# Linear attention differences as products in PSUM, activation tables asked for early, and attention scores in 32-row quarters of the array

## The reference, cut to what matters

```python
def wkv_scan(w, k, v):              # over the tokens of an image, per channel
    def step(carry, kv):
        a, b, m = carry
        mm = maximum(m + w, kt)
        e1 = exp(m + w - mm)
        e2 = exp(kt - mm)
        return (e1 * a + e2 * vt, e1 * b + e2, mm), (a, b, m)
...
M  = maximum(maximum(mf, mb), kt + u)
y  = (exp(mf-M)*af + exp(mb-M)*ab + exp(kk-M)*vt) / (exp(mf-M)*bf + exp(mb-M)*bb + exp(kk-M))
x  = x + sigmoid(h @ Wr_a.T) * y @ Wo_a.T
kf = square(relu(ln(x) @ Wk_f.T))
x  = x + sigmoid(ln(x) @ Wr_f.T) * (kf @ Wv_f.T)
...
attn = softmax(einsum('bhqd,bhkd->bhqk', q, k) * 16**-0.5)
o = einsum('bhqk,bhkd->bqhd', attn, v)
x = x + (o @ proj_w.T + proj_b)
moe = sum over the two best experts e of gate_e * (gelu(ln(x) @ W1[e] + b1[e]) @ W2[e] + b2[e])
```

## Time and profile before

| | us |
|---|---|
| median of 3 runs | 376.76 |
| lowest, highest | 376.1, 378.78 |
| the profiled execution, its own time | 375.74 |
| its span from first to last instruction | 373.9 |
| PE busy | 317.3 (85%) |
| DVE busy | 217.0 (58%) |
| ACT busy | 196.9 (53%) |
| mean granted clock of PE | 0.926 of full |

### The profile page before, as it was taken

How to read it: one execution, slowest core, us unless ns; L and a number is a source line. 1 busy time by engine, 2 the same in 40 slices (tenths; PEclk the granted TensorE clock), 3 DMA queues, 4 the chain that set the end, 5 groups by cost and what they waited for, 6 DMA issues and landing times.

```text
span 373.9 us, 6947 instructions
## 1 busy us (share of the span) xinstructions
PE 317.3 (85%) x2285; PEld 271.7 (73%) x2285; DVE 217.0 (58%) x577; ACT 196.9 (53%) x507; POOL 85.7 (23%) x84
## 2 busy tenths in 40 slices
PE   8959960982199899999999989888899999999990
PEld 5947840672169688797798667778799978889890
DVE  1726998679997684605535467888333434333342
ACT  0053541932847547788966798414365434455550
POOL 9310002002000110100101000011425545546632
PEclk9988995697579999999999999999599999999997
DMA  8960000000000097175731224113213223323332
GB/s 270 356 190 3 0 0 0 3 0 0 0 0 2 1 296 237 38 206 151 227 100 28 75 61 154 39 32 100 69 12 57 45 43 52 53 50 53 53 36 25
DMA packets 23695, 29.13 MB, mean 78 GB/s; under 512 B 6010, under 2 KB 18762, under 8 KB 23658
## 3 DMA queue, kind: packets, MB, share of 16 engines
q1 hardware_dynamic: 19770, 23.85, 21.2%
q0 software_dynamic: 3888, 4.81, 8.1%
HBM read 23.54 MB, written 5.11 MB: 77 GB/s over the span
## 4 chain that ended last, share of the span: by engine, by line
PE 40%; DVE 23%; DMA 12%; issue 11%; ACT 8%; POOL 2%; DVEq 1%; POOLq 1%; SPq 0%; ACTq 0%
DMA out<-s,ffn 10%; PE banks L1284 8%; PE banks L1285 7%; PE banks L1515 4%; PE banks L1366 4%; PE banks L1314 3%; ACT patch L814 3%; PE banks L1498 2%; PE banks L1422 2%; PE banks L1393 2%; PE banks L1410 2%; DVE st L941 2%; PE banks L1329 2%; PE banks L1503 1%; POOL rs L618 1%
## 5 line engine op out<-in xcount | busy, mean ns | idle before, releaser
L618 POOL TENSOR_TENSOR rs<-va,consts 96x6 f32<-96x6 f32 (+1 forms) x16 | 19.1, 1193 | 213.4 <-DVEq L953 109.2
L1515 PE MATMUL banks<-arena,ffn 128*128 x240 | 42.8, 328 | 0.0
L650 POOL DMA_INDIRECT out<-s,ffn x20 | 31.8, 1589 | 45.4 <-DVE s L1241 39.2
L1515 PEld LDWEIGHTS banks<-arena,ffn 128*128 128x128 f32 x240 | 38.5, 190 | 0.5 <-issue 0.2
L874 ACT ACTIVATE ffn<-banks,chans 128x128 f32<-128x128 f32 x21 | 9.6, 458 | 53.6 <-PE banks L1488 50.9
L1329 PE MATMUL banks<-consts,xh 96*128 96x96 f32 (+1 forms) x96 | 12.6, 275 | 22.9 <-ACT xh L700 19.4
L1329 PEld LDWEIGHTS banks<-consts,xh 96*128 96x128 f32 (+1 forms) x96 | 10.0, 142 | 26.1 <-issue 24.7
L640 POOL DMA_INDIRECT vs<-xh_scratch,ffn x21 | 22.3, 1062 | 16.8 <-DVE ffn L1208 8.5
L1366 PE MATMUL banks<-rvw,ffn 128*96 128x192 f32 x144 | 25.4, 327 | 0.5 <-ACT ffn L786 0.5
L1314 PE MATMUL banks<-arena,patch 128*96 128x192 f32 x144 | 25.0, 327 | 0.3 <-DMA patch<-in_xp 0.3
L1314 PEld LDWEIGHTS banks<-arena,patch 128*96 128x96 f32 x144 | 23.0, 162 | 2.3 <-issue 1.9
(11 more groups left out here) (224 smaller groups left out, 771.4 us busy)
## 6 DMA issues: line engine op xcount, KB each, us to landing
arena<-in_w SPq DMA_DIRECT2D x8, 576.0 KB, 7.1
patch<-in_xp SPq DMA_DIRECT2D x12, 288.0 KB, 6.1
arena<-in_w1a SPq DMA_DIRECT2D x8, 384.0 KB, 6.7
vs<-v_scratch SPq DMA_DIRECT2D x24, 114.8 KB
arena<-in_w1b SPq DMA_DIRECT2D x16, 96.0 KB, 5.6
v_scratch<-vt SPq DMA_DIRECT2D x4, 229.5 KB, 2.8
xh_scratch<-xh SPq DMA_DIRECT2D x4, 216.0 KB, 2.4
out<-h SPq DMA_DIRECT2D x1, 864.0 KB
```

Of the source, the lines that this page charges most:

```text
L618: pool.tensor_tensor(dst, src, const_("power", T)[:, 0:n * GTILES], ALU.pow).then_inc(rstd_ready, 1)
L650: pool.indirect_dma_start(out[:, :], bass.IndirectOffsetOnAxis(ap=IS[:, j:j + 1], axis=0), YG[j % 2], None, compute_op=ALU.add).then_inc(s ...
L1515: ins = mm(ps[:, 0:C], HST[j % 2][:, 128 * k:128 * (k + 1)], W2[:, bass.ds(e, 1), C * k:C * (k + 1)], start=(k == 0), stop=(k == HB - 1))
```

## The change

Linear attention. `sub:c:w` (w = 0 to 3) are new jobs: the four differences of part 1 are made by PE, each as three pairs of products of 288 columns, identity times one term plus minus-identity (`MINUS`, made on POOL) times the other, summed in PSUM; ACT takes the exponential straight out of PSUM in three pieces. Part 1 and 2 of `wkv` on DVE keep the other five operations. The order of the exponentials is now e2 before e1. `rc` is Abs_reciprocal_sqrt and Square in place of Ln and Exp, and one-element activations (into a spare column of `KB`) ask for the tables of Tanh at the start, of Abs_reciprocal_sqrt in `rc` ahead of its wait, and of Gelu ahead of the experts.

Ordinary attention. The keys are spread by the parity of the head only: two copies for b=0 and two for b=1 (`spread`). The scores come from `sc:b:g`, for a whole group: 32 channels, which are two heads, are one quarter of the rows of the array, and a product has 32 rows, 64 columns (the queries of one image) and 72 moving columns (its 36 keys for the even and for the odd head). `sc:0` is 32 products into four banks, `sc:1` 16 into two. A job `s:n` (n = 0 to 23, six to a group) is one quarter for all eight images, 288 score columns; DVE and ACT treat it as before. The transposes `pt` of a group wait for all its six exponentials; the probabilities have a buffer for two groups inside `patch`.

Order. PE gets fillers before `kvr:0:0` (4) and `kvr:0:1` (3); `kvr:1:0` moves up ahead of `turn:a:1`; `wexp:0:5` (the Tanh) and `kvr:2:1` move back behind `tok:11`; the scans of chunk 1 move ahead of `wo:0`; `base:0` and `base:1` move up ahead of the last group's end; the norms `22` and `23` are applied on ACT.

```diff
-tok:0 tok:1 tok:2 stats:a:0 tok:3 tok:4 apply:a:0 tok:5 turn:a:0 kvr:0:0 stats:a:1 apply:a:1 turn:a:1 kvr:0:1 wkv:0:0
-kvr:1:0 kvr:1:1 wkv:0:1 wexp:0:0 wexp:0:1 wkv:0:2 wexp:0:2 wexp:0:3 wexp:0:4 wkv:0:3 tok:6 tok:7 wkv:0:4 wkv:0:5 tok:8
-stats:a:2 tok:9 kvr:2:1 tok:10 tok:11 kvr:2:0 stats:a:3 wexp:0:5 apply:a:2 apply:a:3 turn:a:2 turn:a:3 wkv:0:6 rc:0
-wkv:0:7 kvr:0:2 kvr:0:3 wo:0 hx:0 wo:1 kvr:2:3 hx:1 stats:2:0 wkv:1:0 wkv:1:1 apply:2:0 kvr:1:3 kvr:1:2 kvr:2:2
...
+tok:0 tok:1 tok:2 stats:a:0 apply:a:0 tok:3 tok:4 tok:5 turn:a:0 kvr:0:0 kvr:1:0 stats:a:1 apply:a:1 turn:a:1 kvr:0:1
+wkv:0:0 kvr:1:1 tok:6 sub:0:0 sub:0:1 sub:0:2 wexp:0:0 wexp:0:1 wkv:0:1 wkv:0:2 wkv:0:3 wexp:0:2 sub:0:3 wexp:0:3
+wexp:0:4 tok:7 wkv:0:4 wkv:0:5 tok:8 tok:9 tok:10 tok:11 kvr:2:0 stats:a:2 stats:a:3 apply:a:2 kvr:2:1 apply:a:3
+turn:a:2 turn:a:3 wexp:0:5 wkv:0:6 rc:0 wkv:0:7 kvr:0:2 kvr:0:3 wkv:1:0 kvr:1:2 kvr:2:2 wo:0 wo:1 kvr:1:3 wkv:1:1
+sub:1:0 sub:1:1 wexp:1:0 wexp:1:1 sub:1:2 sub:1:3 hx:0 hx:1 stats:2:0 apply:2:0 wexp:1:2 wexp:1:3 wkv:1:2 wexp:1:4
...
-FILL = "logits:2=3 turn:g:3=5 logits:3=3 rank=6 list=14 xt:0=5"
+FILL = "kvr:0:0=4 kvr:0:1=3 logits:2=3 turn:g:3=5 logits:3=3 rank=6 list=14 xt:0=5"
...
-ON_ACT = "a2 a3 20 21"
+ON_ACT = "a2 a3 20 21 22 23"
...
+            pool.tensor_scalar(MINUS[:, :], const_("ident"), -1.0, 0.0, ALU.mult, ALU.add).then_inc(minus_ready, 1)
...
+            A(KB[:, NH:NH + 1], CH[:, 0:1], ACT.Tanh)
...
+                        if c:
+                            act.wait_ge(den_ready, c)
+                        x = here({"e1f": E1F, "e2f": E2F, "e1b": E1B, "e2b": E2B}[what])
+                        for i in range(3):
+                            job = ("sub", c, step[2], i)
+                            src = full(act, job)[:, 0:GT].rearrange("p (i t) -> p i t", t=NT)
+                            dst = x[:, GI * i:GI * (i + 1), :]
+                            if what[1] == "1":
+                                ins = A(dst, src, ACT.Exp, bias=WU[:, i // 2:i // 2 + 1])
+                            else:
+                                ins = A(dst, src, ACT.Exp)
+                            freed(ins, job)
...
+                    A(KB[:, NH:NH + 1], WU[:, 0:1], ACT.Abs_reciprocal_sqrt)
                     act.wait_ge(den_ready, c + 1)
-                    ch.step(A(seed, den, ACT.Ln))
-                    A(seed, seed, ACT.Exp, scale=-1.0).then_inc(seed_ready, 1)
+                    ch.step(A(seed, den, ACT.Abs_reciprocal_sqrt))
+                    A(seed, seed, ACT.Square).then_inc(seed_ready, 1)
...
-                    for h in range(heads):
-                        ins = A(ke[:, :, h, :], src, ACT.Identity, bias=KB[0:rows, 8 * b + h:8 * b + h + 1],
-                                scale=const_(f"head{b}", rows)[:, h:h + 1])
+                    for e in range(2):
+                        ins = A(ke[:, :, e, :], src, ACT.Identity, bias=KB[0:rows, 2 * b + e:2 * b + e + 1],
+                                scale=PAR[0:rows, e:e + 1])
...
+            A(KB[:, NH:NH + 1], CH[:, 0:1], ACT.Gelu)
...
                 if part == 1:
-                    ready(TTR(here(E1F), before(MF), here(MF), ALU.subtract))
-                    ready(TTR(here(E2F), here(k), here(MF), ALU.subtract))
-                    ready(TTR(here(E1B), behind(MB), here(MB), ALU.subtract))
-                    ready(TTR(here(E2B), here(k), here(MB), ALU.subtract))
...
-            def score(p):
+            def score(n):
+                gg, r = divmod(n, NR)
+                ps = full(dve, ("s", n))[:, 0:GI * NT].rearrange("p (h k) -> p h k", h=GI)
+                ch.step(RED(MX[:, n % 2, :], ps, AX.X, ALU.max))
...
+                elif kind == "sub":
+                    c, w = step[1:]
+                    pe.wait_ge(minus_ready, 1)
+                    pe.wait_ge(scan_ready, 2 * c + 1 + w // 2)
+                    m = (MF, MB)[w // 2]
+                    plus = here(K[c]) if w % 2 == 0 else (before(MF), behind(MB))[w // 2]
+                    for i in range(3):
+                        images = slice(GI * i, GI * (i + 1))
+                        job = ("sub", c, w, i)
+                        ps = begin(job)[:, 0:GT].rearrange("p (i t) -> p i t", t=NT)
+                        mm(ps, ident, plus[:, images, :], start=True, stop=False)
+                        end(mm(ps, MINUS[:, :], here(m)[:, images, :], start=False, stop=True), job)
...
-                    for a in range(2):
-                        i = 2 * q + a
-                        mm(ps[64 * a:64 * a + 64, 0:8 * NT], QT[:, gg % 2, 0, NT * i:NT * i + 64], ke0[:, i, :], start=True, stop=True)
...
+                    for q in range(GI // 2):
+                        for a in range(2):
+                            i = 2 * q + a
+                            for r, job in enumerate(jobs):
+                                rows = slice(32 * r, 32 * r + 32)
+                                ins = mm(ps[r][64 * a:64 * a + 64, 2 * NT * q:2 * NT * (q + 1)], QT[rows, g % 2, b, NT * i:NT * i + 64],
+                                         KE[g % 2][rows, b, 2 * NT * i:2 * NT * (i + 1)], start=True, stop=True)
+                                if i == GI - 1:
+                                    end(ins, job)
...
-                    pe.wait_ge(p_ready, p + 1)
+                    gg, q = divmod(p, GI // 2)
+                    pe.wait_ge(p_ready, NR * (gg + 1))
```

More of the change, by code:

```diff
@@ L36 @@
 SW = HS * HW
+NR = C // 32
 E = 8
@@ L110 @@
+spread:1:3 exp:15 vt:3 exp:16 s:17 exp:17 sc:0:3 s:18 s:19 s:20 s:21 turn:g:1 pt:8 pt:9 pv:8 pt:10 exp:18 exp:19
+exp:20 vm:1:2 logits:1 pv:9 pt:11 sc:1:3 s:22 vl:0:3 exp:21 s:23 ot:8 ot:9 pv:10 pv:11 vl:1:3 exp:22 exp:23 pt:12
+ot:10 ot:11 pt:13 base:1 proj:2 vm:0:3 pv:12 pv:13 vm:1:3 pt:14 pt:15 ot:12 ot:13 pv:14 pv:15 stats:g:2 apply:g:2
+ot:14 ot:15 proj:3 stats:g:3 turn:g:2 logits:2 apply:g:3 turn:g:3 base:2 base:3 logits:3
 """
@@ L149, in jobs_of @@
         return [("turn", step[1], x, b) for b in range(2)]
+    if kind == "sub":
+        return [("sub", step[1], x, i) for i in range(3)]
     if kind == "kvr":
```

133 lines of the change are left out of this document (69 added, 64 removed).

## The result

| | before | after |
|---|---|---|
| median us (runs) | 376.43 (4) | 362.27 (4) |
| lowest, highest | 375.95, 378.78 | 360.52, 363.54 |
| the profiled execution | 375.74 | 360.52 |
| its span | 373.9 | 358.7 |
| mean granted clock of PE | 0.926 | 0.974 |

The ratio is 0.9609, with a 95% interval from 0.9547 to 0.967. A second set of runs of the changed kernel, on the chip of the later experiments, gives 0.9637 (0.9585 to 0.969); the experiments are set against that one.

The account below looks back on a forecast made before the run. DVE was taken to bound the linear attention and PE ordinary attention. Terms of -11.2 and -5.2 make -16.4 on the profiled 375.7, giving 359.3; the median lies 1.0 above, so 360 us was forecast, range 351 to 372.

Parts of the forecast that it names:

- Start: Up to the first scan: early Tanh load and fillers holding PE at full clock in kvr:0 save 4.0 us.
- Differences to PE: Linear attention: four operations per chunk leave DVE, 3.96 us twice, saving 7.9 us; PE's new products hidden at full clock.
- Rival 1: Sub products at half clock make exponentials late: 385 us for both chunks and start (0.05), about 371 for one chunk (0.10).
- Reciprocal: DVE's wait for ACT's reciprocal: one table load fewer in rc:1 saves 1.3 us; nothing won in rc:0.
- New order: Ahead of ordinary attention: later tok:11, ACT copies before chunk 1's scan and other waits cost 2.0 us.
- Scores on PE: Ordinary attention: a group's score products take 3.3 us in place of 3.56, saving 1.0 us in all.
- lower bound of 2.3: Score products on PE: 2.3 us a group, from pv's pace times the 0.65 factor of 64-row halves.
- rival 4: Ordinary attention: quarters overlap fourfold (2.3 us a group), spreading pays in full, order closes other holes: 352 us; chance 0.15.
- Spreading keys: Ordinary attention: 48 ACT copies become 16, and half of 7.5 us comes back, saving 3.7 us.
- Softmax, hidden: Ordinary attention: DVE's 48 operations at 0.46 us, 22.1 us in place of 19.4, stay hidden.
- Rival 3: Blocked softmax: PE runs dry 3 us a group while DVE does six scores, spreading gain lost: 376 us; chance 0.10.
- The end: End of ordinary attention: base:0 and base:1 leave the chain, saving 0.5 us.

Follow-up runs that it names:

- e3: Changed kernel without the seven fillers ahead of kvr:0:0 and kvr:0:1: 358.73 us, ratio 0.9551.
- e11: Changed kernel without the early activation that asks for the table of Tanh, fillers kept: 363.94 us, ratio 0.9701.
- e2: Changed kernel with the four differences of each chunk back on DVE, no sub products on PE: 366.85 us, ratio 0.9772.
- e4: Changed kernel with the reciprocal as Exp(-Ln(x)) again, without the early table load in rc: 365.09 us, ratio 0.9744.
- e5: Changed kernel with each group's 48 score products issued quarter by quarter: 365.01 us, ratio 0.9743.
- e9: Changed kernel with only the list altered around the scores of group 3: 364.06 us, ratio 0.9726.
- e12: Changed kernel without softmax maximum and subtraction on DVE; ACT's exponentials read PSUM and stand right behind the score products: 365.07 us, ratio 0.9737.
- e7: Changed kernel with twelve key-spreading copies on ACT per group in place of four, same values: 387.72 us, ratio 1.037.
- e10: Changed kernel with DVE taking the maximum of each of the 24 score tiles twice: 371.88 us, ratio 0.9938.
- e6: Changed kernel with each group's 48 score products issued four times over: 395.41 us, ratio 1.0556.

## Why the prediction was right, by its steps

360 was forecast, 362.3 measured, and 359.3 against 360.52 for the profiled execution. By step:

- **Start, -4.0.** Measured -3.5 (31.62 to 28.08), `kvr:0` at full clock as said. The split was wrong: the gains of the load and of the clock are both there without the fillers (e3), and the clock is there without the early load (e11). The clock was mis-sized. The eight products of `kvr:0` took 6.4 us in the kernel before (20.96 to 24.48 and 27.13 to 30.02) and not 7.3, since the first two of `kvr:0:1` still ran at full clock:

```profile
27.69 0.65 PE L1285 MATMUL banks<-ht,kvrw 128*128 128x288 f32 x2
28.18 1.09 PE L1284 MATMUL banks<-ht,kvrw 128*128 128x288 f32 x2
```

They take 4.0 now, 2.4 less instead of 3.4. `kvr:1:0` ahead of `turn:a:1` cost nothing instead of 1.0: it ends as the norm's tiles are ready.
- **Differences to PE, -7.9.** 4.1 in chunk 0 by e2, 6.9 for both by its mark at the end of chunk 1, about 5 in its time. DVE took 24.4 from the scan to the end of part 5, 24.5 forecast. Rival 1 did not come: in the stretch from 80 to 100 us the clock was 0.91 with the products and 0.61 without.
- **Reciprocal, -1.3.** DVE's waits went from 5.3 to 3.4, and undoing it cost 2.2 to 2.5 (e4). `rc:1` waits 1.12, the 1.3 of the forecast. In `rc:0` the wait fell by 0.6 (2.94 to 2.30), where I had expected the Tanh of r to take all of it back. The Trainium skill's 2.66 us for a change of table (ScalarE: Activation LUTs, What ACT_TABLE_LOAD costs) does not show: each load is 1283 ns, as on that page, but the waits of e4 and after differ by 1.2, no more than the load.
- **New order, +2.0.** `stats:a:3` waited 1.53 us for `tok:11`, 0.5 forecast; the scan of chunk 1 waited 0.65 for ACT, 1.1 forecast. In sum `wo:2` started at 115.41, 115 forecast.
- **Scores on PE, -1.0.** The step that failed. From `wo:2` to the logits I add up, for each score instruction, the time from its start to the next start on PE, less what the profile calls idle: 13.4 us before and 6.0 now, -7.4. A group takes 1.5, below the lower bound of 2.3. The failing term is the 0.0375 per instruction taken from `pv`: products in different quarters of the rows start 0.007 apart in bunches and 0.013 on average. Neighbours in one quarter start 0.022 apart (e5), still well under 0.0375 and with 72 columns to `pv`'s 51, so the order of the quarters explains the step from 0.022 to 0.013 and not the rest. Why 32-row products go so much faster than `pv`'s of 108 rows stays open. It is rival 4's first half and more.
- **Spreading keys, -3.7.** Also wrong, in the other direction. The stretch of ordinary attention in the kernel before and in after, columns as in the earlier trace rows:

```profile
125.90:250.00 124.10, 118.09 (x978) 100.32 (x979) 73.91 (x277) 85.08 (x211) 10.35 (x10) 1.00 0.42 124
115.40:235.00 119.60, 111.19 (x1235) 97.61 (x1234) 73.90 (x287) 74.92 (x197) 10.36 (x10) 1.00 0.45 129
```

PE was idle for 6.0 of 124.1 us before and is idle for 8.4 of 119.6 now, 2.4 more. (The 17.6 in the expectations of e9 and e12 counts small gaps between products too.) So nothing is seen to have come in from the copies, and by

```profile
PE banks L1284 <- ACT patch L814: 1.1, 1, 1.1
```

(a wait of PE in the kernel before) there was little to come in: the old list had the copies far enough ahead. In the new list they stand right in front of their products, and twelve cost 27 us (e7). There fewer copies are needed, and not a gain by themselves. ACT's 3% of the chain, on which the step rested, told of links in a chain, not of time that goes away with them.
- **Softmax, hidden.** 0.45 and 0.46 per operation, 0.46 forecast, 21.8 us against 22.1. Hidden, but without reserve: 10.8 us more come out as 11, at least 5.6 of them as waits (e10). Rival 3 in a mild form: of PE's 8.4 us of waits 5.2 lie between 190 and 225 us, one of them

```profile
213.16 0.62 PE L1459 MATMUL banks<-consts,patch 128*108 128x128 f32 x4 [0.90 <-ACT patch L863]
```

but not because of DVE alone (e12). Which hand-over between ACT, DVE and PE would have to be shortened there stays open: two other lists (e9, e12) moved the waits and did not shorten them.
- **The end, -0.5.** Not seen: from the start of `proj:3` to the end of `logits:3` it was 10.6 us before and is 11.5 now, though `base:0` and `base:1` are gone from there. The waits in it are part of the 8.4.

So the forecast of ordinary attention, -5.2 against -4.2 by the marks, came out right by luck, because wrong terms met: 6.4 us too little from PE, against 3.7 and 0.5 that were not there and 2.4 of new waits. The sum for the linear attention, -11 against -10.5 at `wo:2`, was right by its terms: -3.5 to the first scan, -4.1 in chunk 0, +2.0 from there to its division, -5.2 in chunk 1.

No version beat the changed kernel by more than the measurement tells. e3, which has less in it, is at least as good.

## What to carry to other kernels

An engine's share of the chain says that it is a link, not that the time goes if its work goes; the wait of the bounding engine for it (1.1 us here against 11 on the chain) is the better price. When a list is written anew around a cheaper step, ask what each engine has left there: here the new list is tight on PE, ACT and DVE at once, so that extra work on any of them shows in full (40 for 35, 27 for 17, 11 for 11 us, each with a fall of PE's clock in it), while the one run with less work in ordinary attention (DVE's, e12) gave nothing. A change of the list alone can bring such a fall too: look at the clock of a stretch before a longer time is put down to waits. And moving element work to an idle PE paid in the other engine's time (6.9 us by e2's mark); it raised the clock as well, but no time is seen to come from that.

## What the runs showed of the hardware

- 32-row by 64-column products of 72 f32 columns start 0.013 us apart on average when neighbours stand in different row quarters, down to 0.007 in bunches; 0.022 when neighbours share their quarter (e5), where 72 columns at the rate of 288 in 0.245 would be 0.061.
- In long runs of such instructions PE stands still, in e6 six times in one execution: after 116 to 225 of them at about 0.016 us each (and as many weight loads), for 1.8 to 4.6 us, with "issue" as the only cause, and the mean granted clock is 0.90 there. Blocks of 96 in after and of 128 in e6 with other work ahead of them go through.
- A hole in PE of 1.07 us ahead of `kvr:0:0` (e3), or a load of 1.28 us with fillers over part of it (e11), left the clock at 2.4 GHz; in the kernel before, with the load, no fillers and a hole of 2.48 us, the same products ran at 1.2 GHz.
- The table of Tanh that is asked for at the start serves the Identity activations of the first transposes, which otherwise load one themselves (18.92, 1.28 us, e11). Ln and then Exp took a load each (e4), Abs_reciprocal_sqrt and then Square one for both (after).
